# A two-layer transformer block on one core: the projection stage stores its turned high and low rows, and the first local attention loads them

## The reference, cut to what matters

```python
h = shift_token(x)            # second half of the columns comes from the token before
qkv = h @ wqkv                # 256 -> 3 * 512
q, k, v = split(qkv, 3)       # 8 heads of 64
q = l2norm(q) * qs; k = l2norm(k) * ksc
q, k = rotary_xpos(q, k)
o = local_attention(q, k, v)  # window 128: keys of the own block and of the block before
x = x + o @ wo
h = layernorm(shift_token(x)) * lg + lb
a, g = split(h @ w1 + b1, 2)
x = x + (a * gelu(g)) @ w2 + b2
```

## Time and profile before

| | |
|---|---|
| median of the runs | 1919.55 us |
| the profiled execution's own time | 1915.72 us |
| its span, first to last instruction | 1913.6 us |
| TensorE matmul busy | 1816.2 us (95%) |
| VectorE / ScalarE / GpSimd busy | 1462.9 / 1211.3 / 1000.4 us |
| granted TensorE clock, mean | 0.977 of full |
| DMA, mean over the span | 67 GB/s |
| DMA busy, tenths, first five of 40 slices | 8, 9, 8, 3, 6 |

### The profile page before, as it was taken

How to read it: one execution, slowest core, us unless ns; L and a number is a source line. 1 busy time by engine, 2 the same in 40 slices (tenths; PEclk the granted TensorE clock), 3 DMA queues, 4 the chain that set the end, 5 groups by cost and what they waited for, 6 DMA issues and landing times. The chain is left out here.

```text
span 1913.6 us, 37326 instructions
## 1 busy us (share of the span) xinstructions
PE 1816.2 (95%) x12768; PEld 1298.9 (68%) x12768; DVE 1462.9 (76%) x4115; ACT 1211.3 (63%) x2537; POOL 1000.4 (52%) x807
## 2 busy tenths in 40 slices
PE   7979999999998899999997999989999999889998
PEld 6723333333333788888886888868888888778998
DVE  6678888888882899999997544379999999854543
ACT  4606666666666777777776544358777877655553
POOL 5532223223122778777873444367787778444343
PEclk9959999999999999999998999999999999899999
DMA  8983646455430000100022331100000100242222
GB/s 283 306 145 48 79 57 86 65 73 76 60 48 23 15 29 22 29 29 29 22 58 56 104 114 52 34 30 29 29 24 27 29 29 25 65 126 76 79 78 88
DMA packets 142456, 128.10 MB, mean 67 GB/s; under 512 B 31106, under 2 KB 124734, under 8 KB 142014
## 3 DMA queue, kind: packets, MB, share of 16 engines
q1 hardware_dynamic: 141214, 124.68, 28.4%
q10 hardware_dynamic: 1056, 1.05, 0.2%
HBM read 83.46 MB, written 41.96 MB: 66 GB/s over the span
## 5 line engine op out<-in xcount | busy, mean ns | idle before, releaser
L675 ACT ACTIVATE ca_pr<-ca_pS 128x1024 f32<-128x1024 f32 (+3 forms) x384 | 296.5, 811 | 204.9 <-PE ca_pS L589 163.9
L503 POOL TENSOR_SCALAR_AFFINE_SELECT ca_pr<-ca_pr 128x256 f32<-128x256 f32 x256 | 103.2, 406 | 367.5 <-ACT ca_pr L675 363.1
L704 DVE CUSTOM_DVE_ANT_0 ca_masked<-ca_pR,ca_later 128x256 f32<-128x256 f32 (+3 forms) x512 | 235.6, 485 | 44.7 <-PE ca_pR L565 41.6
L565 PE MATMUL ca_pR<-ca_ks,ca_qs 96*128 96x512 bf16 (+3 forms) x768 | 219.5, 344 | 6.8 <-DVEq L760 3.1
L589 PE MATMUL ca_pS<-ca_qs,ca_ks 98*128 98x512 bf16 (+3 forms) x768 | 183.8, 330 | 12.4 <-issue 6.7
L708 DVE TENSOR_REDUCE ca_mx<-ca_pR 128x1 f32<-128x512 f32 x256 | 175.7, 686 | 25.0 <-PE ca_pR L565 23.2
L565 PEld LDWEIGHTS ca_pR<-ca_ks,ca_qs 96*128 96x128 bf16 x768 | 70.5, 97 | 161.7 <-DVE ca_mx L704 90.1
L941 POOL TENSOR_TENSOR wb_tsn<-wb_qk,base 128x512 f32<-128x512 f32 x62 | 136.5, 2223 | 69.0 <-DVE wb_pn L1156 67.6
L941 POOL TENSOR_TENSOR w_tsn<-w_qk,base 128x512 f32<-128x512 f32 x62 | 136.5, 2222 | 69.0 <-DVE w_pn L1156 67.6
L610 PE MATMUL ca_pO<-ca_pr,ca_va 128*32 128x512 f32 (+3 forms) x1536 | 164.5, 500 | 1.6 <-POOL ca_pr L503 0.8
L1012 ACT ACTIVATE w_pe<-w_sm,w_nmax 128x256 f32<-128x256 f32 (+1 forms) x256 | 123.3, 483 | 67.0 <-DVE w_nmax L1146 66.8
(11 more groups left out here) (297 smaller groups left out, 5396.3 us busy)
## 6 DMA issues: line engine op xcount, KB each, us to landing
QKP<-p_parts SPq DMA_DIRECT2D x32, 384.0 KB, 3.6
ca_qs<-QKP SPq DMA_DIRECT2D x96, 128.0 KB, 6.5
ca_ks<-QKP SPq DMA_DIRECT2D x96, 128.0 KB, 7.2
w_xt<-X SPq DMA_DIRECT2D x64, 128.0 KB, 2.2
X<-w_x SPq DMA_DIRECT2D x64, 128.0 KB, 1.7
f_hh<-X SPq DMA_DIRECT2D x32, 256.0 KB, 6.0
X<-p_xn SPq DMA_DIRECT2D x8, 512.0 KB, 4.8
VA<-p_vst SPq DMA_DIRECT2D x8, 512.0 KB, 4.7
```

What stands on the lines that cost most here:

```text
L565: pe.matmul(bank[:, 0:w], qs[0:SHIFT_ROW, u, h, i * P:(i + 1) * P], ks[0:SHIFT_ROW, u, h, k0:k0 + w], start=True, stop=True).then_inc(ring ...
L675: act.activation(pr[:, k % 2, pair, :, 0:w], pS[:, pair, :, 0:w], ACT.Exp, scale=CS).then_inc(p_ready, 1)
L704: dve.tensor_tensor_reduce(masked[:, jb % RING, 0:w], pR[jb % RING][:, 0:w], later[:, 512 - w:512], -1.0, BIG, ALU.add, ALU.min, mx[:, i, ...
```

## The change

A new DRAM tensor `HT` holds the turned rows, two parts (high, low) by two halves of the columns by 128 partitions by 4100 token columns (one blank column ahead of each sequence). The projection stage stores its `thi` and `tlo` of each step there, 512 KB each, after the third group of the step; two stores of 4-byte elements clear the blank columns. `hi_of` and `lo_of` of a step wait until the store of two steps before has landed. The input rows are loaded 4 instead of 6 steps ahead. The causal stage also loads the turned parts of blocks 0 and 1, and no longer `hs`. In the local attention of the first layer `turn_h`, `turned` and `lo_of` return at once; SyncE loads the four pieces (64 KB each) of block w+4 in step w, once the projection of block w+2 has been made; `hs` is not loaded. The second layer works as before.

```diff
 def phase_project
-    AHEAD = 6
+    AHEAD = 4
-            sp.wait_ge(K.made, 1)
+            sp.wait_ge(K.made, 7)
+            for part in range(2):
+                sp.dma_start(HT[part, 1].rearrange("p (g r) -> p g r", r=SEQ + 1)[:, :, 0:1], K.blank[:, :, :],
+                             allow_slow_non_contiguous=True).then_inc(K.zeroed, 16)
...
+            def store_turned(s, j):
+                col = s * SUP * P + s * SUP // TPB + 1
+                for part, (t, done) in enumerate(((thi, t_hi), (tlo, t_lo))):
+                    sp.wait_ge(done, ONE + s + 1)
+                    sp.dma_start(HT[part, :, :, col:col + SUP * P].rearrange("k p c -> p k c"), t[:, j].bitcast(F32))\
+                      .then_inc(turned_stored[j], 16)
             def rest_of(s, j, it):
...
+                    if g == 2:
+                        store_turned(s, j)
...
             for j in range(2):
                 sp.wait_ge(xn_stored[j], ONE + 16 * SUPERS // 2)
-            sp.wait_ge(K.zeroed, 32)
+                sp.wait_ge(turned_stored[j], ONE + 32 * SUPERS // 2)
+            sp.wait_ge(K.zeroed, 64)
...
             def hi_of(s, j):
                 act.wait_ge(t_ready, ONE + s + 1)
+                act.wait_ge(turned_stored[j], ONE + s // 2 * 32)
...
             def lo_of(s, j):
                 dve.wait_ge(t_hi, ONE + s + 1)
+                dve.wait_ge(turned_stored[j], ONE + s // 2 * 32)
 def phase_causal
                 load_scales(sp, W, 0, scales, qk_scales)
+                for w in range(2):
+                    load_turned(sp, W, HT, w, w, w // TPB)
                 place_shift(0, NJ + 1)
 def load_row(sp, W, layer, X, w, j):
-    sp.dma_start(W.hs[:, j], X[bass.ds(r0 - 1, P), P:D]).then_inc(W.sems["x_loaded"][j], 16)
+    if layer:
+        sp.dma_start(W.hs[:, j], X[bass.ds(r0 - 1, P), P:D]).then_inc(W.sems["x_loaded"][j], 16)
+def load_turned(sp, W, HT, w, j, batch):
+    for t, part in ((W.thi, 0), (W.tlo, 1)):
+        for k in range(KD):
+            sp.dma_start(t[:, j % 2, k].bitcast(F32), HT[part, k, :, bass.ds(w * P + batch + 1 - k, P)])\
+              .then_inc(W.sems["turned_loaded"][j % 2], 16)
 def phase_window
+            def turned_rows(w, j, it):
+                sp.wait_ge(S["v_ready"], ONE + w - 1)
+                load_turned(sp, W, HT, w, j, it)
+            if layer == 0:
+                for w in (2, 3):
+                    turned_rows(w, w, 0)
             def step(w, j, it):
...
+                nxt = ahead(w, j, it, 4)
+                if layer == 0 and nxt:
+                    turned_rows(*nxt)
                 sp.wait_ge(S["x1_ready"], ONE + 2 + g0 + w + 1)
...
             def turned(w, j, it):
+                if layer == 0:
+                    return
...
             def lo_of(w, j, it):
+                if layer == 0:
+                    return
...
             def turn_h(w, j, it):
+                if layer == 0:
+                    return
...
             def project(w, j, it):
-                pe.wait_ge(S["t_lo"], ONE + g0 + w + 1)
+                if layer:
+                    pe.wait_ge(S["t_lo"], ONE + w + 1)
+                else:
+                    pe.wait_ge(S["turned_loaded"][j % 2], ONE + (it * 4 + j // 2 + 1) * 64)
+                    pe.wait_ge(S["x_loaded"][j % 4], ONE + (it * 2 + j // 4 + 1) * 16)
```

More of the change, by code:

```diff
@@ L78, in stack_transfers, with phase_project @@
     return out + [(vin[:, u], VA[n // CG, n % CG])]
-def phase_project(nc, K, W, F, x, X, QKP, VA, wqk, wv):
+def phase_project(nc, K, W, F, x, X, HT, QKP, VA, wqk, wv):
     FIRST_AT, FIRST_TURNS = 2, 4
-    AHEAD = 6
+    AHEAD = 4
     with ExitStack() as c:
@@ L112, in phase_project @@
         x_loaded = [sem(f"p1_x_loaded{i}") for i in range(AHEAD)]
-        blocks = [xin[:, 0], xin[:, 1], F.hh[:, 0], F.hh[:, 1], F.x2[:, 0], F.x2[:, 1]]
+        blocks = [xin[:, 0], xin[:, 1], F.hh[:, 0], F.hh[:, 1]]
         stats = sem("p1_stats")
@@ L117, in phase_project @@
         xn_stored, part_stored, v_stored = K.stored
+        turned_stored = [sem(f"p1_turned_stored{i}") for i in range(2)]
         t_ready, t_hi, t_lo = sem("p1_t_ready"), sem("p1_t_hi"), sem("p1_t_lo")
@@ L174, in rows_of @@
                 if s + AHEAD < SUPERS:
-                    sp.dma_start(blocks[s], x_t[s + AHEAD]).then_inc(x_loaded[s], 16)
+                    sp.dma_start(blocks[s % AHEAD], x_t[s + AHEAD]).then_inc(x_loaded[s % AHEAD], 16)
             def step(s, j, it, final):
@@ L196, in _ @@
                                    base=0, pattern=[[-1, P]], channel_multiplier=1).then_inc(K.made, 1)
+            pool.memset(K.blank[:, :, :], 0.0).then_inc(K.made, 1)
             pool.sem_inc(part2, CG)
@@ L370, in _, with phase_causal @@
             steps(pe, first, step)
-def phase_causal(nc, K, W, X, QKP, VA, AO, wqkv, qk_scales):
+def phase_causal(nc, K, W, X, HT, QKP, VA, AO, wqkv, qk_scales):
     ITERS = BATCH * CG
@@ L832, in score_place, with phase_window @@
     return 2 * (h // 4) + h % 2, h // 2 % 2
-def phase_window(nc, K, W, F, layer, X, wqkv, wo, qk_scales, w1, ln_g, ln_b, b1):
+def phase_window(nc, K, W, F, layer, X, HT, wqkv, wo, qk_scales, w1, ln_g, ln_b, b1):
     NW = TILES
@@ L1273, in project @@
                         pe.wait_ge(S["v_copied"], ONE + g0 + w)
-                        if w == 0:
-                            pe.wait_ge(S["t_lo"], ONE + g0 + 2)
+                        if layer and w == 0:
+                            pe.wait_ge(S["t_lo"], ONE + 2)
                     cols = slice(z * INNER, (z + 1) * INNER)
@@ L2005, in program @@
         K.zeros = sb("zeros", [(2 * LAYERS + 1) * BATCH, D], F32)
+        K.blank = sb("blank", [P, BATCH, 1], F32)
         K.masks = sb("masks", [P, 2, 2 * P], F32)
@@ L2053, in program @@
                         for n, k in (("xn_stored", 2), ("part_stored", CG), ("v_stored", 2))]
-            phase_project(nc, K, W, F, x, X, QKP, VA, wqk, wv)
-            phase_causal(nc, K, W, X, QKP, VA, AO, wqkv, qk_scales)
+            phase_project(nc, K, W, F, x, X, HT, QKP, VA, wqk, wv)
+            phase_causal(nc, K, W, X, HT, QKP, VA, AO, wqkv, qk_scales)
         for layer in range(LAYERS):
@@ L2061, in program @@
                     window_tensors(nc, cw, W)
-                    phase_window(nc, K, W, F, layer, X, wqkv, wo, qk_scales, w1, ln_g, ln_b, b1)
+                    phase_window(nc, K, W, F, layer, X, HT, wqkv, wo, qk_scales, w1, ln_g, ln_b, b1)
                 with ExitStack() as cf:
```

14 lines of the change are left out of this document (8 added, 6 removed).

## The result

| | before | after |
|---|---|---|
| median, lowest to highest of 5 runs | 1919.55 us, 1914.76 to 1920.72 | 1935.53 us, 1932.68 to 1941.41 |
| ratio, 95% interval | | 1.0092, 1.0079 to 1.0106 |
| profiled execution, own time | 1915.72 us | 1935.53 us |
| span | 1913.6 us | 1933.8 us |
| TensorE matmul busy | 1816.2 us (95%) | 1812.9 us (94%) |

The change makes the kernel 0.9% slower, 16.0 us between the medians. The prediction was 1931 us in 1922 to 1946, with slower at 0.86. The two profiled executions lie 20.2 us apart in their spans, because that of before is one of its kernel's faster ones (another one of the same kernel had a span of 1915.2 us).

The account below looks back on a forecast made before the run. Up to the first scores one stream of transfers was taken to bound the kernel, then a loop of engines in the local attention. Losses 19.4 + 1 + 0.9 = 21.3 us less 9.7 gained: 11.6 us slower, median 1931, range 1922 to 1946.

Parts of the forecast that it names:

- What bounds the start: From about 22 to 133 us, up to the first scores, one first-in-first-out stream of transfers sets the time.
- Its price per MB: Projection: the 8.39 MB of turned-row stores move at 370 GB/s, so 22.7 us of DMA time.
- the rows four ahead: Projection: two input loads of 524 KB fall out of the first 20 us into the full part, 2.8 us more.
- Rival A: Projection: the stores hide beside the other transfers, so the kernel is 6 us faster, 1913.5 us; chance 0.06.
- rival B: Projection: TensorE's waits bring the clock to 1.2 GHz, +24 us, 1955; or unaligned stores at half rate, +22 us; chance 0.13.
- The holes: Projection: idle DMA filled by the new stores, -6.1 us; a new 1 us hole at SyncE's end of the projection.
- nothing beyond the stream itself: Projection: the added waits of ScalarE and DVE for stores of two steps before cost nothing extra.
- The causal start: Causal stage's start: eight loads of 64 KB come in, four `hs` loads go, 0.9 us more ahead of `place_shift`.
- The local attention: First layer: 0.27 us gained per block, 7.8 us for 29 blocks, plus 1.9 us at the start: 9.7 us.
- has slack in the steady step: Local attention: second maxima, residual and normalising, held back by `lo_of` on DVE, have slack; exponentials run without gap.
- rival C: Local attention: DVE's missing 0.34 us counts too, 0.71 us per block, 22.5 us with the start; 1918.5 us; chance 0.07.
- Rival D: Local attention: turned-row loads come late and TensorE waits for `turned_loaded`, 1 us per block, 32 us, 1963; chance 0.02.

Follow-up runs that it names:

- the high half alone: Changed kernel storing only the high part of the turned rows, loaded in place of the low part too: 1926.93 us, ratio 1.0045.
- the third buffer: Changed kernel with three instead of two buffers for `thi` and `tlo`, so copies wait for the store of three steps before: 1938.27 us, ratio 1.0095.
- the one with the stores alone: Kernel before with the changed kernel's whole projection stage and the old local attention, which never reads `HT`: 1941.74 us against 1918.85, ratio 1.0121.
- the kernel with the loads alone: Changed kernel without stores of turned rows, input rows six ahead, loads of the same size reading `X`: 1916.85 us, ratio 0.9984.
- the addition first: Changed kernel with GpSimd's rotation addition issued ahead of the inverse norms in both layers: 1918.26 us against 1919.33, ratio 1.0002.
- two kernels that both have the addition there: Addition ahead of the inverse norms: in the changed kernel, 1918.26 us; in the kernel before, with `place_shift` also ahead of the loads that follow it, 1910.56 us.
- moving one line: `place_shift` issued ahead of loads needed only later: in the kernel before 1913.01 us, ratio 0.9967; in the changed kernel 1931.82 us, ratio 1.0069.

## Why the prediction was right, and where it was wrong

**What bounds the start: right.** One stream of transfers up to the first scores. Its price per MB was 2.65 us where 2.70 was put, the rows four ahead cost 2.6 us (2.8), the end of the stream is `place_shift`. Rival A, that the stores hide, is refuted by the share of 1.01 to 1.08 and by the high half alone. The half of rival B that has the unaligned stores slow is refuted by the 2.65 us per MB.

**The holes: mis-sized by about 2 us.** The first maxima came 22.8 us later and the first causal load 22.5 us, where 22.7 + 2.8 - 6.1 + 1 = 20.4 was put. The stretch from 20 us to that load, before (to 96 us) and after:

```profile
20.00:96.00 76.00, 70.37 (x427) 61.49 (x425) 51.37 (x111) 49.38 (x86) 45.60 (x47) 1.00 0.92 293
```

```profile
20.00:118.50 98.50, 75.40 (x427) 64.11 (x425) 51.63 (x110) 49.81 (x86) 44.87 (x47) 0.93 1.00 326
```

Against the full 1.06, the DMA time in it is 76 x 0.92 / 1.06 = 66.0 us before and 98.5 x 1.00 / 1.06 = 92.9 us after: 26.9 us more, where 25.5 was put. The rest is holes: 10.0 us before, 5.6 after, so 4.4 us were filled net, not 5.1. Together that is 22.5. The claim that the waits for `turned_stored` were "nothing beyond the stream itself" was nearly right in what they cost (the third buffer brought the scores forward by 1.1 us), but the forecast of a share of 1.05 to 1.09 up to the barrier was not: at 102 and 112 us it was 0.68 and 0.73. The first of these holes lies in the second stretch at the low clock; what leaves them was not tested. The miss of 2 us is no larger than the scatter between kernels with the same projection stage: the one with the stores alone had the maxima at 116.7 us, 20.3 us later than before, which is the 20.4 of the forecast.

**The clock, rival B's other half.** It happened, and cost far less than the 24 us that the rival had: after waits of 4.2 and 4.3 us the products ran at the 1.2 GHz level for about 5 and 3.4 us, and the mean clock from 20 to 118.5 us was 0.93. Nineteen products that took 0.43 us instead of 0.24 are 3.6 us of TensorE's time, an estimate; how much of that reached the barrier was not measured. TensorE's busy time from 20 us on rose from 70.4 to 75.4 us for the same 427 matmuls, within a stretch that had 17.5 us more of idle (23.1 us against 5.6).

**The causal start: right in the whole.** It was put at 0.9 us; from the first causal load to the scores it is 38.30 us against 37.68, 0.6 us more, with 1.5 us in the kernel with the loads alone.

**The local attention: wrong by 5.4 us.** Forecast 9.7, measured 4.3. The step that failed is "what it held back (second maxima, residual, normalising) has slack in the steady step", and with it the choice of 0.24 to 0.37 us a block. The scores did come earlier and the maxima did stop waiting for them. But the step has a second loop, which doesn't pass through the scores: sum of squares on VectorE, inverse norm and addition on GpSimd (0.25 + 2.92 + 2.40 us), normalising on VectorE, which ends 0.94 us after the addition (814.53 and 813.59 us), then the second four, the unit rows and the next sum of squares. In the changed kernel that takes 819.27 - 806.54 = 12.73 us (start of the sum of squares to the next), just under the 12.84 of the old loop. Halving or moving the addition shortened it, and did nothing in the steady block of the kernel before, which is what shows it. Before, the addition ended at 804.86 us and the four at 805.79, with 0.93 us between them too; VectorE's row there:

```profile
803.98 1.81 DVE L1156 TENSOR_SCALAR w_pn<-w_pe,w_rsum 128x256 f32<-128x256 f32 x4
```

Taking 0.37 us of TensorE and 0.34 us of VectorE out of the old loop could only gain the difference. The blocks gave 1.5 us instead of 7.8, the start 2.8 instead of 1.9.

With the second loop opened (the addition first), the change gains 431.4 - 414.6 = 16.8 us in this stage, two kernels that both have the addition there; 3.1 us of it lie in the last two steps (27.3 and 24.3 us), which scatter. That is more than the forecast's own bounds allowed (10.7 + 1.9), barely so without these 3.1 us, and less than rival C's 22.5. The steady step fell from 12.83 to 12.41 us, 0.42 us, where rival C had 0.71. So with GpSimd out of the way a little more than TensorE's 0.37 us counts; whether the rest is the missing VectorE time is not shown.

**Rival D: refuted.** No wait for `turned_loaded` appears in the local attention, and the loads land in 2.0 us (median).

**The number.** The losses were 22.8 + 0.3 us instead of 21.3, the gain 4.3 instead of 9.7, scatter of the causal stage +1.4: 20.2 in the spans where 11.6 was put. The median moved by less, 16.0, because the profiled execution of before lies 3.8 us under its median and that of after on its median. So 4.5 us of error are left against 1931, inside the range. That is in part luck: the stages add up to 8.6 us of error, of which the choice of the profiled executions takes back 4.

## What to carry to other kernels

A store that goes into a stage with a full DMA costs its bytes over the full rate, here 2.65 us per MB, and one more buffer for it gave back 1.1 us at most; and what gates the next stage belongs ahead of the loads that nobody needs yet (moving one line brought the first scores forward by 6.6 and 8.0 us). When work is taken out of one engine's loop, walk the other loops of the step before pricing the gain: here one of 12.73 us lay behind the one of 12.84. Moving one GpSimd instruction ahead of another then gave 17 us, and nothing that could be told apart in the kernel before.

## What the runs showed of the hardware

Four `tensor_scalar` of 128x256 in fp32, SBUF to SBUF, took 1.14 us alone on VectorE and 2.18 us when GpSimd's `tensor_tensor` of 128x1024 (2.40 us) ran into them. It is the first of the four that waits, as the view of the changed kernel's `w_pn` from 812 to 814.5 us shows (durations in ns, shortest, median, longest):

```profile
L1198 DVE TENSOR_SCALAR w_pn<-w_pe,w_rsum x4: 341/342/1392, 812.3 to 814.2; 128x256 f32<-128x256 f32 x4
```

It took 1.39 us and ended 0.15 us after the addition; the other three took their usual 0.34 us, overlapping. In the 30 other blocks of the layer in which the two meet, the first one ends 0.09 to 0.33 us after the addition too. The Trainium skill, "SBUF — State Buffer", section "Who interferes with whom", says that the two engines share a pair of ports as an exclusive lock, held for the whole instruction, and that `tensor_scalar` can be in a mode that needs it. The wait for the addition agrees. The length of the lock doesn't for every instruction: with the addition moved, GpSimd's power on 128x16 (from 805.43 us, 2.92 us long) was running when the same four started at 807.41 us, and they took 1.14 us.

The 2 KB rows of the new stores, 4 to 16 bytes off a round address and 16.4 KB apart, cost 2.65 us per MB (378 GB/s) in the full stage, no slower than the 371 to 385 GB/s read from the kernel before. And single waits of 4.2 and 4.3 us between two groups of matmuls were followed by the 1.2 GHz level for about 5 and 3.4 us.
